# The scatter of the experts' rows, moved from a stage of its own into the attention's batch loop

## The reference, cut to what matters

```python
x = qz                                   # (8, 512, 128)
xn = layernorm(x)
# layer 0: attention by ternary factors, 16 channels of 64, and experts, both added to x
u, v = xn @ U.T * s, xn @ V.T * s        # split in 16 channels
q = sigmoid(u @ v.T)                     # 512 x 512 for each channel
attn = (q @ v) @ U * s + (q.T @ u) @ V * s
vals, idx = top_k(sigmoid(xn @ Wr.T), 64)            # 64 tokens for each of 8 experts
y[e] = causal_attention(rope(xn[idx[e]] @ Wqkv[e])) * vals[e] @ Wo[e]
experts = zeros.at[idx].add(y)                       # the scatter
x = x + attn + experts
# layer 1: linear attention with a hierarchical mask, then a gated feed-forward, both on layernorm(x)
```

## Time and profile before

| | us |
|---|---|
| median of 3 runs | 1660.54 |
| lowest, highest | 1657.77, 1664.48 |
| the profiled execution | 1660.13 |
| its span, first to last instruction | 1657.5 |

### The profile page before, as it was taken

One profiled execution on the slowest core, in us unless ns is written; L12 is line 12 of the kernel. 1 busy time (PEld: TensorE's weight loads), 2 busy tenths in 40 slices (PEclk: granted clock), 3 DMA queues, 4 the chain that ended last, 5 costly groups with the idle time before them and its releaser, 6 DMA issues.

```text
span 1657.5 us, 25450 instructions
## 1 busy us (share of the span) xinstructions
PE 1532.5 (92%) x8464; PEld 874.7 (53%) x8464; DVE 858.2 (52%) x1549; ACT 770.8 (47%) x1172; POOL 56.5 (3%) x45
## 2 busy tenths in 40 slices
PE   3799699999999999999999999999999999999977
PEld 1666565555555555555555555555555555555544
DVE  8767732335554455445454554455444554454546
ACT  1246045555544554455444544455445544554431
POOL 5100400000000000000000000000000000000000
PEclk8799899999999999999999999999999999999988
DMA  6002000000000000000000000000000000000000
GB/s 193 1 27 60 13 1 1 1 1 1 1 1 8 2 1 1 1 9 1 1 1 8 1 1 1 8 1 1 1 7 2 1 1 1 9 1 0 1 7 7
DMA packets 19835, 15.79 MB, mean 10 GB/s; under 512 B 1504, under 2 KB 18016, under 8 KB 19584
## 3 DMA queue, kind: packets, MB, share of 16 engines
q1 hardware_dynamic: 19376, 12.17, 2.6%
q0 software_dynamic: 336, 1.97, 0.3%
HBM read 9.94 MB, written 2.10 MB: 7 GB/s over the span
## 4 chain that ended last, share of the span: by engine, by line
issue 86%; PE 6%; DVE 6%; POOL 1%; ACT 1%; DMA 0%; SPq 0%; DVEq 0%; POOLq 0%; ACTq 0%
PE psum L1086 5%; DVE arena L791 0%; DVE arena L625 0%; DVE small L624 0%; DVE arena L797 0%; DVE upper L559 0%; DMA x_all<-in_x 0%; DVE upper L575 0%; DVE upper L680 0%; DVE upper L678 0%; DVE upper L687 0%; DVE upper L689 0%; ACT arena L920 0%; DVE upper L676 0%; DVE upper L674 0%
## 5 line engine op out<-in xcount | busy, mean ns | idle before, releaser
L1008 ACT ACTIVATE th_second<-psum 128x1024 f32<-128x1024 f32 x256 | 248.9, 1023 | 436.7 <-PE psum L1086 436.7
L1008 ACT ACTIVATE arena<-psum 128x1024 f32<-128x1024 f32 x258 | 250.4, 1025 | 209.4 <-PE psum L1086 194.1
L735 DVE TENSOR_SCALAR o_hl<-psum,sums 128x512 fp32r<-128x512 f32 x128 | 96.1, 750 | 409.5 <-PE psum L1086 409.5
L1086 PE MATMUL psum<-arena 128*64 128x512 f32 (+2 forms) x1280 | 279.2, 541 | 11.6 <-DVE arena L843 11.6
L1086 PE MATMUL psum<-th_second,arena 128*64 128x512 f32 x1024 | 241.4, 592 | 0.0
L1086 PE MATMUL psum<-v_parts,u_parts 64*128 64x512 f32 (+1 forms) x1568 | 220.6, 407 | 0.0
L1086 PE MATMUL psum<-u_parts,v_parts 64*128 64x512 f32 x1548 | 214.4, 408 | 4.7 <-issue 3.4
L1086 PEld LDWEIGHTS psum<-v_parts,u_parts 64*128 64x128 f32 (+1 forms) x1568 | 140.7, 184 | 96.7 <-issue 73.2
L1086 PEld LDWEIGHTS psum<-u_parts,v_parts 64*128 64x128 f32 x1548 | 135.8, 184 | 96.5 <-issue 64.8
L920 ACT ACTIVATE arena<-psum 128x512 f32<-128x512 f32 (+4 forms) x228 | 127.2, 589 | 115.0 <-PE psum L1086 48.3
L1086 PEld LDWEIGHTS psum<-arena 128*64 128x64 f32 (+1 forms) x1280 | 93.0, 149 | 131.2 <-issue 131.2
(11 more groups left out here) (183 smaller groups left out, 1661.9 us busy)
## 6 DMA issues: line engine op xcount, KB each, us to landing
x_all<-in_x SPq DMA_DIRECT2D x4, 512.0 KB, 5.8
upper<-in_we SPq DMA_DIRECT2D x8, 256.0 KB, 2.7
arena<-upper SPq DMA_DIRECT2D x16, 128.0 KB, 2.5
out<-x_all SPq DMA_DIRECT2D x8, 256.0 KB, 2.4
arena<-in_e POOLq DMA_DIRECT2D x1, 1216.0 KB, 5.8
arena<-in_wi POOLq DMA_DIRECT2D x1, 576.0 KB, 6.4
uT_w<-in_uT SPq DMA_DIRECT2D x1, 512.0 KB, 6.6
vT_w<-in_vT SPq DMA_DIRECT2D x1, 512.0 KB, 6.4
```

Source lines behind the costliest of these rows:

```text
L735: nc.vector.tensor_scalar(o_hl[:, o, 0], o_bank[:], total, None, ALU.add).then_inc(s_oh, 1)
L1008: nc.scalar.activation(th_of(un), psum[:, at:at + 2], ACT.Tanh, scale=0.5 * FACTOR_SCALE ** 2).then_inc(s_th, 2)
L1086: return nc.tensor.matmul(out, lhsT, rhs, start=start, stop=stop)
```

## The change

- The expert rows go to a DRAM scratch `expert_rows` instead of `y_all`. For each batch SP loads its 512 rows into `xn_s`, a tile that layer 1 uses only from half 1 to half 2 of the next batch.
- In half 0 of each batch DVE prepares the scatter's operands: rows times pick value, split in two fp32r parts, and four selectors of 0 and 1 in fp32r.
- In half 1, behind `tv`, PE does the scatter transposed: eight accumulating passes of 512 columns into a bank of the middle, where the attention's sum has its form. DVE copies it to `gT`, and all eight projections are added to it. The stage between experts and attention is gone, and so are its add to `x_all` and the float32 products.
- The pick positions and values of all batches are taken out once, ahead of the experts.
- The four first preparations use three banks instead of one. POOL's splits are ordered in three pairs (uT and vT; gate and up; u and v), and each wait for them stands at its first user: `prep` k = 1 (two splits), `project` and the first `evac_o` (all six).
- The store of batch n - 1 stands on SP behind the load of the rows of batch n + 1.

```diff
-    preps = [(kind, h // 2) for kind in PREP_IN_HALF[h % 2]]
+    preps = [(kind, h // 2) for kind in PREP_IN_HALF[h % 2]] + [("sc", 0)] * (h == 1)
...
+        y_rows, y_weighted = xn_s, kf32.rearrange("p (e d) -> p e d", e=E // 2)
+        y_hl = [k_stk, q_stk]
+        selT = [sel_r[:, 2], sel_r[:, 3], vl_stk[:], selT_last[:]]
...
+            def load_rows(n):
+                sp.dma_start(y_rows[:], y_dram.ap()[n].rearrange("(e h) q d -> (h q) e d", h=2)).then_inc(s_yl, 16)
...
+            load_rows(0)
+            sp.wait_ge(s_yp, 1)
+            load_rows(1)
+            with sp.Fori(1, B - 1) as n:
+                sp.wait_ge(s_yp, n + 1)
+                wait_emptied(sp, ("norm", 0), n - 1)
+                load_rows(n + 1)
+                store(n - 1)
...
+            split_weights(((uT_w, uv_hl[0]), (vT_w, uv_hl[1])), 0)
+            split_weights(((wg, gu_hl[0]), (wu, gu_hl[1])), 2)
...
+                elif o == 0:
+                    dve.wait_ge(s_parts, 6)
...
-            def weights_back(n, par):
...
-                for e2 in range(E // 2):
-                    ins = nc.vector.tensor_scalar(selT[:, par, e2], tokens[:], iv_s[:, par, 0, e2:e2 + 1], iv_s[:, par, 1, e2:e2 + 1],
-                                                  ALU.is_equal, ALU.mult)
...
+            def scatter_operands(i):
+
+                dve.wait_ge(s_yl, i * 16 + 16)
+                link(nc.vector.tensor_tensor(y_weighted, y_rows[:], pick_value[:, i].unsqueeze(2).broadcast_to([P, E // 2, D]), ALU.mult))
+                link(nc.vector.tensor_copy(y_hl[0][:], kf32[:]))
                 for e2 in range(E // 2):
+                    nc.vector.tensor_scalar(selT[e2], tokens[:], pick_at[:, i, e2:e2 + 1], None, ALU.is_equal)
+                nc.vector.tensor_tensor(y_hl[1][:], kf32[:], y_hl[0][:], ALU.subtract).then_inc(s_yp, 1)
+
+            def start_g(i):
+                dve.wait_ge(s_scat, i + 1)
+                nc.vector.tensor_copy(gT[:], x_bank(("sc", 0))[:]).then_inc(s_scf, 1)
...
+                    if isinstance(g, int) and g == 0 and k == 1:
+                        pe.wait_ge(s_parts, 2)
...
+            def scatter(i, bk):
+
+                pe.wait_ge(s_yp, i + 1)
+                for e2 in range(E // 2):
+                    for part in range(2):
+                        ins = mm(bk[:], y_hl[part][:, e2 * D:(e2 + 1) * D], selT[e2], e2 == part == 0, e2 == E // 2 - 1 and part == 1)
+                ins.then_inc(s_scat, 1)
...
             for k in range(1, 5):
-                if k > 1:
-                    pe.wait_ge(s_prep_free, k - 1)
-                prep(-1, k, 0, 0, x_banks[0])
+                if k == 3:
+                    pe.wait_ge(s_ys, E)
+                if k == 4:
+                    pe.wait_ge(s_prep_free, 1)
+                prep(-1, k, 0, 0, x_banks[(k - 1) % X_BANKS])
...
-            pe.wait_ge(s_ffn, B)
...
-            pe.wait_ge(s_parts, 6)
             pe.wait_ge(s_x1, 1)
             pe.wait_ge(s_prep_free, 4)
```

More of the change, by code:

```diff
@@ L144, in is_prep @@
 def is_prep(work):
-    return work[0] in ("pu", "pv", "pj", "tu", "tv")
+    return work[0] in ("pu", "pv", "pj", "tu", "tv", "sc")
 def bank_user_before(work, among):
@@ L199, in build @@
         u_hl, v_hl = (sb(n, [P, 2, 2, T], F32R) for n in ("u_parts", "v_parts"))
-        k_stk, q_stk, vl_stk = (sb(n, [P, T], F32R) for n in ("k_stk", "q_stk", "vl_stk"))
+        k_stk, q_stk, vl_stk, selT_last = (sb(n, [P, T], F32R) for n in ("k_stk", "q_stk", "vl_stk", "selT_last"))
         stats = sb("stats", [P, TB, 6])
@@ L219, in view @@
             return a
-        ARENA, UPPER = 14848, 6924
+        ARENA, UPPER = 14400, 6924
         arena = sb("arena", [P, ARENA])
+        KEPT = ARENA - T - 2 * B * (E // 2)
+        tokens = arena[:, ARENA - T:ARENA]
+        pick_at, pick_value = (view(arena[:, lo:lo + B * (E // 2)], (B, E // 2)) for lo in (KEPT, KEPT + B * (E // 2)))
         early = ExitStack()
@@ L250, in build @@
         csg = take(E, B, KSEL)
-        y_all = take(B, E // 2, D)
+        at[0] += 2 * E * B * KSEL // 2
         rvT = take(2, TB, E * B)
@@ L254, in build @@
         iota1 = take(KSEL)
-        tokens = take(T)
         picks = take(B, (E // 2) * NPICK)
-        iv_s = take(2, 2, E // 2)
         token_at = take(TB)
         causal = take(P)
-        we, wo_e = take_upper(2, EW - P), take(2, P)
+        assert at[0] <= KEPT
+        we, wo_e = take_upper(2, EW - P), view(arena[:, 3 * E * B * KSEL - 2 * P:3 * E * B * KSEL], (2, P))
         mark = at_upper[0]
@@ L340, in build @@
         s_qk_hi, s_xgs = sem("qk_passed_rows"), sem("picked_copied")
-        s_selw, s_scat, s_ffn = (sem(n) for n in ("selT_ready", "scattered", "ffn_added"))
+        s_yl, s_yp, s_scat, s_scf = (sem(n) for n in ("expert_rows_loaded", "expert_rows_split", "scattered", "scatter_copied"))
         s_chain = sem("dve_chain")
@@ L441, in move_rows @@
                 for half in range(2):
-                    sp.dma_start(y_all[64 * par:64 * par + 64].rearrange("p (q r) e d -> p q r e d", r=2)[:, :, half, ep, :],
+                    sp.dma_start(y_dram.ap().rearrange("(a r) (e h) q d -> r h e q a d", r=2, h=2)[half, par, ep],
                                  y_s[64 * half:64 * half + 64, par]).then_inc(s_ymv[par], 16)
@@ L457, in _, with store @@
                 move_rows(E - 2 + par, E // 2 - 1, par)
-            with sp.Fori(0, B) as n:
+            def load_rows(n):
+                sp.dma_start(y_rows[:], y_dram.ap()[n].rearrange("(e h) q d -> (h q) e d", h=2)).then_inc(s_yl, 16)
+            def store(n):
                 wait_emptied(sp, ("down", 0), n)
                 sp.dma_start(io["out"][n].rearrange("(k p) d -> p k d", p=P), x_all[:, n]).then_inc(s_st, 16)
+            for par in range(2):
+                sp.wait_ge(s_ymv[par], 16 * E)
+            load_rows(0)
[6 more added lines that the diff above has]
+                store(n - 1)
+            store(B - 2)
+            store(B - 1)
             sp.wait_ge(s_st, 16 * B)
@@ L500, in _, with split_weights @@
             pool.wait_ge(s_ymv[1], 16 * E)
[L501 to L509, removed]
-            pool.wait_ge(s_prep_full, 2)
[L511 to L515, removed]
+            def split_weights(pairs, done):
+                for w, parts in pairs:
+                    pool.tensor_copy(parts[:, 0], w[:]).then_inc(s_hi, 1)
+                pool.wait_ge(s_hi, 4 + done + len(pairs))
+                for w, parts in pairs:
+                    pool.tensor_tensor(parts[:, 1], w[:], parts[:, 0], ALU.subtract).then_inc(s_parts, 1)
+            split_weights(((uT_w, uv_hl[0]), (vT_w, uv_hl[1])), 0)
+            split_weights(((wg, gu_hl[0]), (wu, gu_hl[1])), 2)
+            pool.wait_ge(s_parts, 4)
+            pool.wait_ge(s_prep_full, 2)
+            split_weights(((u_w, w_hl[0]), (v_w, w_hl[1])), 4)
             with pool.Fori(0, B) as n:
@@ L656, in _ @@
             dve.wait_ge(s_gx, B)
+            nc.vector.tensor_copy(pick_at[:], picks.rearrange("p b (e s) -> p b e s", s=NPICK)[:, :, :, 0])
+            for h in range(2):
+                rows = slice(64 * h, 64 * h + 64)
+                high, low = (picks[rows, :, base:base + (E // 2 - 1) * (NPICK + 2) + 1:NPICK + 2] for base in (2 + h, 2 + E + h))
+                nc.vector.tensor_tensor(pick_value[rows], high, low, ALU.add)
             def expert_rows(n, par, m):
@@ L722, in add_g @@
                 dve.wait_ge(s_pj_full, i * PAIRS + j)
[L723 to L727, removed]
+                nc.vector.scalar_tensor_tensor(gT[:], bk[:], 0.5 * FACTOR_SCALE ** 2, gT[:], ALU.mult, ALU.add).then_inc(s_pj_free, 1)
             def evac_o(g, j, o, some_before):
@@ L857, in _ @@
             split_rows(0)
[L860 to L870, removed]
+            dve.wait_ge(s_prep_w, 1)
             nc.vector.memset(bs6[64:128], 1.0)
-            dve.wait_ge(s_parts, 6)
             def iteration(i, attn, second):
@@ L886, in iteration @@
                     some_before = second or j
+                    if h == 0:
+                        scatter_operands(i)
                     for work in MIDDLE[h]:
-                        if work[0] == "pu":
+                        if work[0] == "sc":
+                            start_g(i)
+                        elif work[0] == "pu":
                             prep_u(g, g + 1 if some_before else None, (j + 1) % 2)
@@ L911, in body @@
                 iteration(i, True, True)
-            loop(1, B, 2 * PAIRS + 1 + 2 + 2 + NF + 1, body)
+            loop(1, B, 2 * PAIRS + 1 + 2 + 2 + NF + 1 + 2, body)
             iteration(B, False, True)
@@ L1066, in iteration @@
                             prep_tok(g, 4, v_tok, (j + 1) % 2, q, x_bank(work))
-                        elif work[0] != "pj" and second:
+                        elif not is_prep(work) and second:
                             l1(work, i - 1, x_bank(work))
@@ L1391, in iteration @@
                         kind = work[0]
```

(7 more changed lines are left out.)

38 lines of the change are left out of this document (6 added, 32 removed).

## The result

| | before | after |
|---|---|---|
| median, us | 1661.96 (4 runs) | 1640.12 (4 runs) |
| lowest, highest | 1657.77, 1664.48 | 1637.90, 1642.11 |
| the profiled execution; its span | 1660.13; 1657.5 | 1642.11; 1640.3 |

The change makes the kernel 1.24% faster: ratio 0.9876, 95% interval 0.9860 to 0.9892. Forecast were 1636 us and a range of 1631 to 1646.

What follows compares the result with a forecast made beforehand. PE was taken to bound the batch loop, while the start ahead of it held little that the attention needs. 1660.13 less 39.0 us at the start plus 14.7 in the loop gave 1635.8, so 1636 us, range 1631 to 1646.

Steps and rivals of the forecast that it cites:

- PE bounds the loop, and the rest there is covered: Batch loop: work added to PE costs full length, 2.1 us per batch, 14.7 us in all; DVE's additions cost nothing.
- the cover of 0.8 us: Half 1 of a batch: slack left at the output bank's evacuation, queued behind the later layer 1 statistics; no cost.
- DVE in half 0: Half 0 of each batch: 3.7 us of scatter operands ahead of prep_u fit in DVE's idle time and cost nothing.
- the first scores at 175 to 177: Start of attention: PE's first scores matmul no longer waits for any weight split and starts then instead of at 219.
- the mark: Start of batch 0's fifth weighted unit, the first with tanh values of pair 0's second half; from 234.26 to 195.3.
- the factor 3: Start: DVE's slowdown beside POOL's weight splitting, from 15.8 us spent on work that takes 5.3 us elsewhere.
- 182.1 + 11.0 + 1.9: PE's chain at the start: first two weight splits done, PE's work from that preparation, batch 0's scatter; ends at 194.9.
- DVE's chain: Start: DVE's scatter operands, then prep_u and prep_v, done at 193.8; the scores behind them end at 195.5.
- A: Rival at the start: PE's low clock costs 2.3 us, DVE blocked twice more 2.5 each; 1639 to 1642 us; chance 0.11.
- B: Rival in half 1: late statistics or evacuation make PE wait one or two us per batch; about 1650 us; chance 0.09.
- C: Rival in the loop: scatter passes run at four-byte speed, 8.4 us per batch; 1680 us, slower than before; chance 0.03.
- D: Rival at the start: PE finds no work it can do before 193, so 206 instead of 195.3; 1647 us; chance 0.05.

Runs made afterwards that it cites:

- the copies: Changed kernel with one or six more DVE copies of the scatter's bank to gT in each batch: 1640.10 and 1656.80 us.
- The seven traces: Traces of seven kernels with the changed kernel's DVE and POOL start code unmoved: first scores 179.28 to 184.42, fifth weighted unit of batch 0 at 198.50 to 202.46.
- rows early: Changed kernel with the split of batch 0's rows moved ahead of the last expert's scaling: 1639.21 us, ratio 0.9878 to the kernel before.
- the two better starts: Changed kernel with batch 0's row split and selectors ahead of the last expert's scaling, without and with ACT making three high parts: 1637.60 and 1636.23 us.
- ACT's casts: Changed kernel with batch 0's row split and selectors ahead of the last expert's scaling, and ACT making three high parts: 1636.23 us, ratio 0.9848 to before.
- all splits first: Changed kernel with the first scores again waiting for all six weight splits, the scatter still in the loop: 1652.59 us, ratio 0.9956 to before.

## Why the prediction was right, and where it was not

- *PE bounds the loop, and the rest there is covered.* Right. A batch is 2.1 us longer, as the sum had it, and from the mark to the end there are 14.8 us more against 14.7. The trace of after, half 1 of a batch:

```profile
523.47 0.69 DVE L794 TENSOR_TENSOR x_all<-psum,x_all 128x512 f32 x1 [0.75 <-PE psum L1339]
...
524.29 0.49 PE L1092 MATMUL psum<-sel_r,k_stk 128*128 128x512 f32 x1
...
526.02 0.40 PE L1092 MATMUL psum<-selT_last,q_stk 128*128 128x512 f32 x1
526.35 1.66 PE L1092 MATMUL psum<-u_parts,v_parts 64*128 64x512 f32 x12
526.46 0.69 DVE L867 COPY arena<-psum 128x512 f32<-128x512 f32 x1 [2.29 <-PE psum L1092]
...
531.64 0.75 DVE L760 TENSOR_SCALAR o_hl<-psum,sums 128x512 fp32r<-128x512 f32 x1 [0.84 <-PE psum L1092]
```

  The first pass starts 0.13 us after DVE's add of "back" ends, the eight passes take 2.06 us to the next scores, and the evacuation still waits 0.84 us for PE: the cover of 0.8 us was right, and the copies bear it out.
- *DVE in half 0.* The result (nothing) was right, its working was not. The new operands start at 513.95, 2.44 us after the evacuation, and only "issue" stands before them:

```profile
513.95 0.69 DVE L859 TENSOR_TENSOR arena<-xn_s,arena 128x512 f32<-128x512 f32 x1 [2.44 <-issue]
...
521.18 0.75 DVE L760 TENSOR_SCALAR o_hl<-psum,sums 128x512 fp32r<-128x512 f32 x1 [0.88 <-PE psum L1092]
```

  The loop's back edge stands between the two in DVE's program, and the wait is most likely for instructions. Before, the same stretch looked like a wait for ACT, and I took it for room. The prediction had all done at 548, 2.7 us ahead of the evacuation. In the trace of before DVE stood idle 3.81 us for PE in front of it:

```profile
550.72 0.75 DVE L735 TENSOR_SCALAR o_hl<-psum,sums 128x512 fp32r<-128x512 f32 x1 [3.81 <-PE psum L1086]
```

  Of that, 0.88 us are left in the trace of after.
- *The start.* The step that failed, though the total came out, is "the first scores at 175 to 177", that is the mark at 195.3. I had laid the factor 3 on the operands and on prep_u and prep_v, and had named the split of batch 0's rows in the same list, but gave it no price and let PE's chain begin before it. PE's first scores wait for it. So in the trace of after the chain was not 182.1 + 11.0 + 1.9, but 184.16 + 5.3 for the first scores at the low clock + 12.85 = 202.3. The seven traces show the wait (first scores from 179.3 to 184.4, marks from 198.5 to 202.5), and "rows early" and the two better starts that behind it DVE's chain (with 197.8) and then PE's (with 197.6 and 196.7) come next. DVE's chain was too short in the sum as well: prep_v was to be out at 193.8, and the evacuation behind it started at 197.31 in the trace of after and at 196.05 with the rows early. Even the best start stays above 195.3, since the experts end later than in the first trace and part of PE's first work runs at 1.2 GHz.
- *The rivals.* What happened at the start is A, by its mechanism: DVE blocked twice more and the clock low, with a mark of 202 beyond its 201. The total, 1640.12, lies inside the forecast's own range of 1632 to 1641 all the same, and inside A's 1639 to 1642. So the forecast is right by the loop's term and by the width of its range, and in part by luck: with the start as it was, its own sum gives 1660.13 - 32.0 + 14.8 = 1642.9 (the profiled execution took 1642.11). The low clock had been ruled out because "no pause in my plan is longer than 2.5 us"; the pause was 7.34. Nor would the shorter pauses have kept the clock: with ACT's casts PE paused 1.03, 0.68 and 1.55 us between 175 and 183, and the clock was 0.79 from 182 to 184 and 0.50 from 184 to 186. B and C did not occur. D did not occur either; "all splits first", which puts its wait back, costs 12 us.
- *POOL's split* ended at 194.7 against 193.1, and the DMAs did as forecast: the moves to DRAM land in 2.5 us, the rows' load in 2.8.

The lock rule of the Trainium skill (page "SBUF — State Buffer", "Who interferes with whom") is borne out by the traces of the start: in the runs above a DVE cast or subtraction beside a POOL subtraction of 1024 columns takes 2.4 to 2.9 us, POOL's length and not its own. Laid on the split of batch 0's rows it would have given that split a price, 2.7 us beside POOL's casts and 5.3 beside its subtractions by the table above. Which of the two it is hangs on less than a microsecond, so it could have given the range of the first scores and not one time.

## What to carry to other kernels

When a stage is taken out, list every wait of the first instruction behind it, and give each waiting instruction its length in the company that it will have there, not the length that it has elsewhere. A wait for a group of results, moved to the first user of each, can be worth more than half of what the work removed is (12 against 21 us here, and only with both together); but an early start only pays if the engines that feed it aren't blocking each other. Where an engine bounds a loop, work added to it costs its full length, and slack of the others is to be read behind the loop's back edge too, where an idle stretch may be the wait for instructions. And where engines hold each other up, one trace of a start is not enough: the same code had its mark anywhere in 4 us.

## What the runs showed of the hardware that was not expected

- Eight or sixteen matrix products placed ahead of the loop made each batch inside it 2.8 or 3.7 us longer, by a second wait behind the back edge (1.36 to 1.92, and 2.23 to 2.25 us, for at most 0.38) and, in the second case, a clock at 0.50 after it. Here a straight piece of code cost more in the loop behind it than where it stood; why is argued above and not shown.
- In the experts' stage, seen at 164 to 172 us, the clock fell to 0.50 in thirteen of fourteen traces and stayed at 1.00 in one. That one and one of the thirteen are of the same program, the kernel before.
- Two products of the first preparation that took 1.92 us for 1.02, at the low clock, went with first scores 4.4 us later: DVE's two instructions behind them then met two POOL subtractions (2.56 and 2.71 us) and not two casts (1.26 and 1.41).
